# Layer-norm statistics of a hybrid block: row sums taken with the residual additions, squared distances on ScalarE

## The chip, the cores and the metric

The kernel runs on one core of a Trainium2 chip. The metric is the device time of one launch in microseconds. Before the change three runs gave a median of 2213.21 us (2209.37 to 2219.28).

The engines are named as in the profile: PE is TensorE, PEld its weight loads, DVE is VectorE, ACT is ScalarE, POOL is GpSimd, SP is SyncE (it issues DMAs only). Each takes its own instructions strictly in order and waits for the others by semaphores.

## The reference

Input x has 16 batches of 512 tokens with 256 features, float32. One block of a hybrid network is applied, with four residual steps and a layer norm (no weights) in front of each:

```python
x = x + attention(layernorm(x))   # 16 heads, causal, RMS norm first, returns xn + out
x = x + ffn(layernorm(x))         # base + shared low-rank + top 2 of 6 routed low-rank
x = x + ssm(layernorm(x))         # conv of 4 taps, silu, softplus, scan with 16 states, gate
x = x + ffn(layernorm(x))

def layernorm(x, eps=1e-05):
    m = mean(x, -1); v = var(x, -1)
    return (x - m) / sqrt(v + eps)
```

The change concerns the mean and variance of the second, third and fourth of these layer norms.

## The kernel before, in words

A batch is held as a tile X of 128 partitions by 4 token blocks by 256 features; five such slots rotate. All engines walk through one common calendar. A group of four heads is a step q; a step has UN = 10 units p, and a unit has two places, 2(10q + p) and one more. Four groups make a batch, so the calendar repeats every 80 places. The tables PE_AT, ACT_AT, DVE_AT, POOL_AT and SP_AT say at which place, counted from the start of a batch's attention, an engine does each piece of side work for that batch (its projections, norms, feed-forward, state-space part). `due` (L239) picks the batch whose turn it is, `side_work` of each engine runs down its list. Some five batches are in flight: attention of one, feed-forward of the one before, the scan of an earlier one. The places are only an order of instructions on each queue. Time follows from the semaphores.

Between the side work stands the fixed work of each unit. PE makes scores twice: for the row maxima (L357, L359), 14 units ahead, into two PSUM banks that DVE reduces (L970 to L975), and for the exponentials (L380, L382), into two banks that ACT reads (L767); then products with the values (L405). DVE runs one scan of the state (L1090) and one product with the row C (L1097) four times per step; ACT makes the decays for them (L864), POOL the input products (L1262), and POOL's DMA adds each state's product to y (L1269). Two more PSUM banks, MA and MB, serve all side work; BANK says which result lies in which, and a bank is filled again only when its reader has freed it.

A layer norm goes through three engines. There are four kinds: q before attention, f and l before the first and the last feed-forward, s before the state-space part. For f, s and l:

- DVE adds the PSUM result of the step before to X, two token blocks at a time (`add_to_x`, L1016 to L1020: places add_x1, add_up0, add_x3).
- `moments_of_sum` (L1022) waits for both halves and calls `moments` (L1003): four bn_stats, four bn_aggr, then the variance with epsilon into `va` and the negative mean into `ng` (L1013, L1014). Its places are stats_f, stats_s and stats_l.
- POOL's `rsqrt` (L1227) raises `va` to the power -0.5 into `rs` (L1229) and multiplies by `ng` into `nm` (L1231).
- ACT's `normalise` (L774) writes X times rs plus nm for four token blocks (L777). PE then transposes.

Kind q has its statistics from DVE as well, and they stay there. The last feed-forward's result is added by `add_to_x` (add_up1) and stored by SP (`store`, L722), which waits for both halves. SP's queue also carries the loads of stacked q and k parts (`stack`, L687, three thirds at the first three units of a step) and the broadcast rows of B (`load_b`).

Of the kernel before, what the change touches and what calls it, by code (L numbers as in the profile page):

```python
# [56 lines left out]
def hybrid_block(nc, x, norm_w, wqk_t, bqk_c, wv_t, bv, wo_t, bo, conv_w, conv_b, wd_t, bd, wbc_t,  # L57
# [32 lines left out]
    PRODUCT_AT = {1: 0, 4: 1, 6: 2, 8: 3}  # L90
# [6 lines left out]
    PE_AT = {"xn": (-76, -71), "qk00": (-52, -50, -48), "qk01": (-49, -47, -44), "v": (-29, -34),  # L97
# [4 lines left out]
    BANK = {"xn": (0, 1), "qk00": 0, "qk01": 1, "v": (1, 1), "qk10": 0, "qk11": 1, "ao": (1, 1), "x1": (1, 0),  # L102
            "turn0": (1, 1), "low0": 1, "hw0": 1, "up0": (1, 0), "xs": (1, 0), "conv": (1, 1), "gate": (1, 0),
            "bc": 1, "dt": (0, 0), "x3": (1, 0), "turn1": (1, 0), "low1": 0, "hw1": 0, "up1": (1, 0)}
    ACT_AT = {"norm_q": -97, "norm_f": 103, "exp0": 116, "norm_s": 131, "softplus": 152, "decays": 160,
# [4 lines left out]
    DVE_AT = {"add_x1": (94, 96), "stats_f": 98, "in0": 111, "out0": 117, "add_up0": (125, 125), "stats_s": 127,  # L110
              "silu": 143, "delta": 155, "gated": 246, "add_x3": (251, 251), "stats_l": 252, "in1": 265, "out1": 267,
              "add_up1": (279, 282), "stats_q": -100}
    POOL_AT = {"weigh": -57, "residual": -57, "rsqrt_f": 99, "rsqrt_s": 122, "rsqrt_q": -104, "inputs": 151,
               "rsqrt_l": 253, "low": (111, 268)}
    SP_AT = {"parts": (-42, -3), "load_x": -109, "store_b": 144, "store": 280}
# [3 lines left out]
    with ctx:  # L119
# [77 lines left out]
        nm = sb("nm", [P, 4, TB])  # L197
        low = sb("low", [P, 2, TB, LR])
# [558 lines left out]
        def _(act):  # L757
# [115 lines left out]
            def side_work(now):  # L873
# [46 lines left out]
                if (a := due(now, ACT_AT["norm_q"])) >= 0:  # L920
                    act.wait_ge(res_done.sem, res_done.at(a - 1))
                    normalise(a, KIND_Q, X[:, a % XS, :, :], tok_q)
                if (a := due(now, ACT_AT["norm_f"])) >= 0:
                    normalise(a, KIND_F, X[:, a % XS, :, :], tok_f)
                if (a := due(now, ACT_AT["exp0"])) >= 0:
                    exp_logits(a, 0)
                if (a := due(now, ACT_AT["norm_s"])) >= 0:
# [3 lines left out]
                if (a := due(now, ACT_AT["decays"])) >= 0:  # L931
                    decays(a, 0)
                    decays(a, 1)
                if (a := due(now, ACT_AT["norm_l"])) >= 0:
# [26 lines left out]
        def _(dve):  # L961
# [41 lines left out]
            def moments(b, kind, mul, add):  # L1003
                src = X[:, b % XS, :, :]
# [145 lines left out]
            def side_work(now):  # L1150
# [3 lines left out]
                for j in range(2):  # L1154
                    if (a := due(now, DVE_AT["add_x3"][j])) >= 0:
                        add_to_x(a, side["x3", j], ("x3", a, j), j)
                if (a := due(now, DVE_AT["stats_l"])) >= 0:
                    moments_of_sum(a, KIND_L, ("x3",))
# [7 lines left out]
                for j in range(2):  # L1166
                    if (a := due(now, DVE_AT["add_x1"][j])) >= 0:
                        if j == 0:
                            dve.wait_ge(res_done.sem, res_done.at(a))
                        add_to_x(a, side["x1", j], ("x1", a, j), j)  # L1170
                if (a := due(now, DVE_AT["stats_f"])) >= 0:
                    moments_of_sum(a, KIND_F, ("x1",))
# [4 lines left out]
                for j in range(2):  # L1177
                    if (a := due(now, DVE_AT["add_up0"][j])) >= 0:
                        add_to_x(a, side["up", 0, j], ("up", a, 0, j), j)
                if (a := due(now, DVE_AT["stats_s"])) >= 0:  # L1180
                    moments_of_sum(a, KIND_S, ("up", 0))
# [22 lines left out]
            for q in range(FIRST, END):  # L1204
# [3 lines left out]
                for p in range(UN):  # L1208
                    if 0 <= UN * q + p + LM < UN * NQ:
                        maximum(UN * q + p + LM)  # L1210
                    if p == HEADS_DVE and 0 <= q - 1 < NQ:
                        head_norm(q - 1)
# [5 lines left out]
                    if p == 6 and 0 <= q + 1 < NQ:  # L1218
# [145 lines left out]
```

## Time and profile before

| | |
|---|---|
| median of three runs | 2213.21 us |
| the profiled execution | 2220.23 us |
| its span, first to last instruction | 2218.4 us |
| mean granted TensorE clock | 0.934 of full |
| PE busy | 1819.8 us, 82% |
| DVE busy | 1856.9 us, 84% |
| ACT busy | 1289.4 us, 58% |
| POOL busy | 1171.1 us, 53% |

Busy time is the sum of an engine's instruction durations, in which short overlaps of neighbours count twice. So a slot, the distance between two starts, is often shorter than a duration. A wait names the instruction that was kept waiting, then the one whose end released it. Line numbers are those of the kernel before.

### The profile page before, as it was taken

The numbers are of one execution on the slowest core, as the hardware profiler recorded it, in microseconds if no ns is written. First come the engines' busy times: TensorE is split into PE (matmuls) and PEld (weight loads), VectorE is DVE, ScalarE is ACT, GpSimd is POOL, SyncE is SP. The second block draws the span as 40 slices with busy tenths as digits, with TensorE's granted clock in tenths as the row PEclk, the third lists the DMA queues.
The fourth block names the chain that finished last, engine by engine and source line by source line (L and its number), as shares of the span: only waits on it lengthen the run. The fifth ranks groups of instructions, "written<-read, shape, count | busy, mean of one in ns | idle before, by whom it ended". The sixth has DMA issues, their size and how long they took to land.

```text
span 2218.4 us, 32220 instructions
## 1 busy us (share of the span) xinstructions
PE 1819.8 (82%) x10881; PEld 1082.1 (49%) x10912; DVE 1856.9 (84%) x2760; ACT 1289.4 (58%) x2260; POOL 1171.1 (53%) x994
## 2 busy tenths in 40 slices
PE   5789787888889798888888788888978888877775
PEld 2445444546355454645455454545545463535343
DVE  5444798989899897989899898989889897978784
ACT  2446566566756657575665656576565657463531
POOL 1110665656455564647465464756556474556682
PEclk8999899999989999999999899999999999888988
DMA  4312576667657665666767666666766666651110
GB/s 114 91 49 68 120 152 145 145 140 152 130 125 155 140 153 124 146 137 137 154 134 147 143 145 136 140 130 142 151 143 152 129 149 129 124 120 53 48 62 14
DMA packets 186054, 275.56 MB, mean 124 GB/s; under 512 B 33554, under 2 KB 125731, under 8 KB 185891
## 3 DMA queue, kind: packets, MB, share of 16 engines
q1 hardware_dynamic: 155650, 163.40, 28.9%
q0 software_dynamic: 30240, 110.11, 26.8%
q8 instruction: 87, 1.43, 0.3%
q14 instruction: 77, 0.62, 0.1%
HBM read 128.72 MB, written 34.08 MB: 73 GB/s over the span
## 4 chain that ended last, share of the span: by engine, by line
PE 31%; DVE 26%; DMA 14%; issue 12%; ACT 8%; POOL 5%; SPq 3%; DVEq 0%; POOLq 0%; ACTq 0%
DVE hc L1090 9%; PE bank L313 7%; DMA y<-hc 5%; DVE hc L1097 4%; POOL inp L1262 4%; PE bank L322 4%; DMA sk<-qk_parts 3%; DMA qk_parts<-parts 3%; PE bank L503 3%; PE bank L357 2%; PE bank L486 2%; PE bank L405 2%; PE bank L380 2%; DVE mall L975 2%; SPq L698 2%
## 5 line engine op out<-in xcount | busy, mean ns | idle before, releaser
L1262 POOL TENSOR_TENSOR inp<-u,b_all 128x512 f32<-128x512 f32 x512 | 731.8, 1469 | 333.7 <-DVE hc L1090 222.0
L1090 DVE TENSOR_TENSOR_SCAN hc<-dec,inp 128x1024 f32<-128x1024 f32 x256 | 672.4, 2627 | 20.7 <-ACT dec L864 19.3
L767 ACT ACTIVATE pt<-bank 128x512 f32<-128x512 f32 x640 | 375.2, 598 | 253.0 <-PE bank L382 251.1
L357 PE MATMUL bank<-sk,sq 96*128 96x512 bf16 (+3 forms) x1024 | 281.7, 314 | 131.9 <-DVE mall L973 52.3
L1269 POOL DMA_DIRECT2D y<-hc x210 | 186.0, 886 | 353.9 <-DMA y<-hc 162.5
L864 ACT ACTIVATE dec<-dt,a_neg 128x511 f32<-128x511 f32 x512 | 338.5, 719 | 39.4 <-DVE hc L1090 39.4
L1097 DVE TENSOR_TENSOR hc<-hc,bank 128x1024 f32<-128x1024 f32 x242 | 293.3, 1212 | 25.5 <-PE bank L542 24.9
L380 PE MATMUL bank<-sq,sk 98*128 98x512 bf16 (+3 forms) x1024 | 276.4, 308 | 15.3 <-DMA sq<-hlt 10.3
L973 DVE TENSOR_REDUCE mall<-bank 128x1 f32<-128x512 f32 x256 | 172.5, 674 | 138.6 <-PE bank L359 138.4
L357 PEld LDWEIGHTS bank<-sk,sq 96*128 96x128 bf16 x1024 | 102.9, 100 | 279.4 <-DVE mall L973 80.0
L313 PE MATMUL bank<-xt_q,wqk 128*128 128x512 f32 x256 | 153.6, 731 | 73.8 <-ACT bcs L844 67.9
L359 PE MATMUL bank<-mask_qk,ident_bf 128*128 128x128 bf16 x1024 | 199.9, 226 | 0.0
L382 PE MATMUL bank<-mask_kq,ident_bf 128*128 128x128 bf16 x1024 | 197.6, 224 | 0.0
L975 DVE TENSOR_REDUCE mall<-bank 128x4 f32<-128x512 f32 x256 | 172.9, 675 | 19.2 <-PE bank L359 18.9
L405 PE MATMUL bank<-pt,v_sb 128*32 128x512 f32 (+3 forms) x2048 | 186.3, 460 | 0.0
L1229 POOL TENSOR_TENSOR rs<-va,half 128x4 f32<-128x4 f32 x64 | 88.1, 1376 | 185.4 <-DVE ng L1014 185.3
L786 ACT ACTIVATE parts<-bank,bqk 128x512 bf16<-128x512 f32 x192 | 131.2, 688 | 93.7 <-PE bank L313 87.1
L380 PEld LDWEIGHTS bank<-sq,sk 98*128 98x128 bf16 x1024 | 103.7, 101 | 80.2 <-issue 19.6
L542 PE MATMUL bank<-bcs,onehot 96*128 96x512 bf16 x256 | 102.7, 401 | 35.3 <-DVE hc L1097 34.5
L359 PEld LDWEIGHTS bank<-mask_qk,ident_bf 128*128 128x128 bf16 x1024 | 103.5, 101 | 46.2 <-issue 28.4
L382 PEld LDWEIGHTS bank<-mask_kq,ident_bf 128*128 128x128 bf16 x1024 | 103.5, 101 | 42.2 <-issue 25.9
L1019 DVE TENSOR_TENSOR X<-bank,X 128x512 f32<-128x512 f32 x128 | 85.5, 678 | 45.5 <-PE bank L322 25.6
(152 smaller groups left out, 3271.6 us busy)
## 6 DMA issues: line engine op xcount, KB each, us to landing
y<-hc POOLq DMA_DIRECT2D x210, 512.0 KB, 5.5
b_all<-b_kept SPq DMA_DIRECT2D x256, 256.0 KB, 4.3
qk_parts<-parts SPq DMA_DIRECT2D x96, 256.0 KB, 3.1
sq<-qk_parts SPq DMA_DIRECT2D x384, 64.0 KB, 3.4
sk<-qk_parts SPq DMA_DIRECT2D x384, 64.0 KB, 3.6
X<-in_x SPq DMA_DIRECT2D x16, 512.0 KB, 7.9
out<-X SPq DMA_DIRECT2D x16, 512.0 KB, 3.0
sq<-hlt SPq DMA_DIRECT2D x256, 2.0 KB
```

The source lines that it names most:

```text
L313: last = mm(dst[:, :], w[:, c, g * P:(g + 1) * P], src[:, c, :], start=(c == 0), stop=(c == C - 1))
L357: mm(dst[:, o:o + n], sq[0:KS, slot, h, qb * P:(qb + 1) * P], sk[0:KS, slot, h, 0:n], start=True, stop=False)
L359: return mm(dst[:, o + n - P:o + n], ident_bf[:, :], mask_qk[:, :], start=False, stop=True)
L380: mm(dst[:, o:o + n], sk[:, slot, h, kb * P:(kb + 1) * P], sq[:, slot, h, kb * P:T], start=True, stop=False)
L382: return mm(dst[:, o:o + P], ident_bf[:, :], mask_kq[:, :], start=False, stop=True)
L405: last = mm(pv_bank[VW * i:VW * (i + 1), kb * P:T], values_of(a, kb, first + i), pt[:, n % PT, at:at + T - kb * P], start=start, stop=stop ...
L767: A(pt[:, n % PT, :], score_bank[unit % 2][:, :], ACT.Exp).then_inc(exp_done.sem, 1)
L864: last = A(dec[:, n % 2, c, 1:T], dt[:, c, 1:T], ACT.Exp, scale=a_neg[:, c, n:n + 1])
L975: V.tensor_reduce(mall[:, w, h, 0:4], max_bank[m % 2][:, :].rearrange("p (k n) -> p k n", k=TB), AXX, ALU.max).then_inc(mx_done.sem, 1)
L1090: V.tensor_tensor_scan(h, d, v, 0.0, ALU.mult, ALU.add).then_inc(scan_done.sem, 1)
L1097: V.tensor_tensor(hc[:, k % HC, :, :] if n or s >= LATE else y[:, s % 2, :, :], hc[:, k % HC, :, :], spread_bank[:, None, :].to_broadcast( ...
L1262: last = G.tensor_tensor(inp[:, n % 2, c, :], u[:, c, :], b_all[:, k % 3, :], ALU.mult)
```

## The change

The additions for f, s and l now take each token block by itself, in an operation that also sums the row (`add_and_sum`). ACT makes the negative mean from the sums and then the sum of squared distances from it, with an accumulating Square (`squares`); it waits for both additions first. POOL divides by 256 and adds epsilon before the power. The statistics of kind q, and the last addition (add_up1), are as before. `squares` writes its elementwise output into the tile that the norm overwrites. The places and banks of the side work are new.

```diff
+            def squares(b, kind, name, junk):
+                for j in range(2):
+                    m = side[*name, j]
+                    act.wait_ge(m.free, m.at(name[0], b, *name[1:], j))
+                A(ng[:, kind, :], sums[:, kind, :], ACT.Copy, scale=-1.0 / D).then_inc(act_own.sem, 1)
+                act.wait_ge(act_own.sem, act_own.one())
+                for tb in range(TB):
+                    last = A(junk[:, tb, :], X[:, b % XS, tb, :], ACT.Square, bias=ng[:, kind, tb:tb + 1],
+                             accum_out=va[:, kind, tb:tb + 1])
+                last.then_inc(var[kind].sem, 1)
...
-            def moments_of_sum(b, kind, name):
-                for j in range(2):
-                    m = side[*name, j]
-                    dve.wait_ge(m.free, m.at(name[0], b, *name[1:], j))
-                moments(b, kind, 1.0, 1e-5)
+            def add_and_sum(b, m, name, j, kind):
+                dve.wait_ge(m.full, m.at(*name))
+                for t in range(2):
+                    row = X[:, b % XS, 2 * j + t, :]
+                    last = V.scalar_tensor_tensor(row, m.tile[:, t * D:(t + 1) * D], 1.0, row, ALU.mult, ALU.add,
+                                                  accum_out=sums[:, kind, 2 * j + t:2 * j + t + 1])
+                last.then_inc(m.free, 1)
...
             def rsqrt(b, kind):
                 pool.wait_ge(var[kind].sem, var[kind].at(b))
+                if kind != KIND_Q:
+                    G.tensor_scalar(va[:, kind, :], va[:, kind, :], 1.0 / D, 1e-5, ALU.mult,
+                                    ALU.add).then_inc(pool_own.sem, 1)
+                    pool.wait_ge(pool_own.sem, pool_own.one())
...
-    PRODUCT_AT = {1: 0, 4: 1, 6: 2, 8: 3}
+    PRODUCT_AT = {1: 0, 3: 1, 6: 2, 8: 3}
```

The tables of places, in the entries that the prediction speaks of or that moved most:

| entry | before | after |
|---|---|---|
| ACT square_f, square_s, square_l | none | 98, 125, 252 |
| DVE stats_f, stats_s, stats_l | 98, 127, 252 | gone |
| DVE add_x1, add_x3 | (94, 96), (251, 251) | same |
| DVE add_up0 | (125, 125) | (124, 124) |
| POOL rsqrt_f, rsqrt_s, rsqrt_l | 99, 122, 253 | 97, 122, 254 |
| POOL weigh, residual | -57, -57 | -56, -45 |
| POOL inputs | 151 | 153 |
| PE v | (-29, -34) | (-26, -32) |
| PE turn1 | (260, 262) | (262, 264) |
| PE up0 | (125, 126) | (123, 125) |
| DVE add_up1 | (279, 282) | (277, 280) |
| SP store, load_x, store_b | 280, -109, 144 | 278, -112, 146 |

Most others of attention's projections and both feed-forwards move by one to three; conv, gate, bc, dt, silu and delta stay. The banks of v, ao, x1 and x3 change for one half each. `finish_maxima` stands at the same place as before.

## Rows read from the trace of the kernel before

**Rows 1.** The page, busy time and share by engine, whole span.

```profile
PE 1819.8 (82%) x10881; PEld 1082.1 (49%) x10912; DVE 1856.9 (84%) x2760; ACT 1289.4 (58%) x2260; POOL 1171.1 (53%) x994
```

**Rows 2.** Busy time by stretches: length, PE, PEld, DVE, ACT, POOL, clock, DMA.

```profile
903.00:1029.00 126.00, 106.66 (x672) 65.47 (x673) 116.23 (x171) 80.15 (x141) 73.68 (x64) 0.96 0.67 143
...
1785.00:1911.00 126.00, 106.80 (x664) 64.51 (x666) 112.04 (x161) 77.84 (x137) 71.40 (x62) 0.95 0.66 139
...
925.00:945.00 20.00, 19.68 (x146) 13.89 (x145) 19.61 (x27) 12.13 (x23) 11.02 (x9) 1.00 0.81 181
...
957.00:992.00 35.00, 28.88 (x160) 13.53 (x159) 27.19 (x28) 29.05 (x48) 16.48 (x15) 0.95 0.55 109
```

**Rows 3.** Waits of DVE, 903 to 1029 us: us in total, times, longest.

```profile
DVE mall L973 <- PE bank L359: 4.5, 2, 3.4
DVE mall L970 <- PE bank L359: 1.8, 2, 1.5
```

**Rows 4.** Waits of PE in the same period.

```profile
PE bank L313 <- ACT bcs L844: 4.9, 1, 4.9
PE bank L357 <- DVE mall L973: 3.4, 3, 2.3
PE bank L357 <- DVE mall L975: 2.8, 3, 1.4
```

**Rows 5.** DVE in order of time: start us, us, engine, line, operation.

```profile
1000.66 0.42 DVE L999 TENSOR_TENSOR ao<-bank,rc 128x256 f32<-128x256 f32 x1
1001.01 1.21 DVE L1097 TENSOR_TENSOR hc<-hc,bank 128x1024 f32<-128x1024 f32 x1
...
1014.98 0.68 DVE L1019 TENSOR_TENSOR X<-bank,X 128x512 f32<-128x512 f32 x1
1015.58 1.21 DVE L1097 TENSOR_TENSOR hc<-hc,bank 128x1024 f32<-128x1024 f32 x1
...
1017.31 1.40 DVE L1006 BATCH_NORM_STATS2 st<-X 128x6 f32<-128x256 f32 x4
...
1019.23 0.16 DVE L1014 TENSOR_SCALAR ng<-mv 128x4 f32<-128x4 f32 x1
1019.30 0.69 DVE L970 TENSOR_REDUCE mall<-bank 128x2 f32<-128x512 f32 x1
```

**Rows 6.** By line: durations in ns, min/median/max, then first and last start.

```profile
L1019 DVE TENSOR_TENSOR X<-bank,X x128: 656/680/694, 144.9 to 2214.2; 128x512 f32<-128x512 f32 x128
...
L1108 DVE SCALAR_TENSOR_TENSOR y<-gate,bank x4: 655/678/686, 2110.5 to 2182.9; 128x512 f32<-128x512 f32 x4
```

**Rows 7.** ACT: in order of time, its largest wait of the period, one line's durations.

```profile
936.53 0.59 ACT L793 COPY v_sb<-bank 128x512 f32<-128x512 f32 x1 [5.68 <-PE bank L322]
...
1016.50 0.57 ACT L767 ACTIVATE pt<-bank 128x512 f32<-128x512 f32 x1
...
1022.21 2.07 ACT L777 ACTIVATE tok_f<-X,nm,rs 128x256 f32<-128x256 f32 x4 [0.15 <-POOL nm L1231]
...
ACT pt L767 <- PE bank L382: 15.0, 10, 4.9
...
L947 ACT ACTIVATE a_neg<-a_neg x1: 229/229/229, 36.0 to 36.0; 128x32 f32<-128x32 f32 x1
```

**Rows 8.** POOL, by line: the power and the product of the norm.

```profile
L1229 POOL TENSOR_TENSOR rs<-va,half x64: 1007/1034/2934, 7.1 to 2190.8; 128x4 f32<-128x4 f32 x64
...
L1231 POOL TENSOR_TENSOR nm<-ng,rs x64: 202/203/2251, 8.2 to 2191.8; 128x4 f32<-128x4 f32 x64
```

**Rows 9.** The chain of waits, at the start and at the end.

```profile
148.29 1.41 DVE st L1006 x4
...
2187.78 0.70 DVE X L1019
2188.58 1.42 DVE st L1006 x4
```

**Rows 10.** POOL in order of time, behind the last statistics.

```profile
2191.84 0.20 POOL L1231 TENSOR_TENSOR nm<-ng,rs 128x4 f32<-128x4 f32 x1
```

More of the change, by code:

```diff
@@ L96, in hybrid_block @@
     FRAME = 2 * UN * NG
-    PE_AT = {"xn": (-76, -71), "qk00": (-52, -50, -48), "qk01": (-49, -47, -44), "v": (-29, -34),
[4 rows of a table removed]
-    BANK = {"xn": (0, 1), "qk00": 0, "qk01": 1, "v": (1, 1), "qk10": 0, "qk11": 1, "ao": (1, 1), "x1": (1, 0),
-            "turn0": (1, 1), "low0": 1, "hw0": 1, "up0": (1, 0), "xs": (1, 0), "conv": (1, 1), "gate": (1, 0),
-            "bc": 1, "dt": (0, 0), "x3": (1, 0), "turn1": (1, 0), "low1": 0, "hw1": 0, "up1": (1, 0)}
-    ACT_AT = {"norm_q": -97, "norm_f": 103, "exp0": 116, "norm_s": 131, "softplus": 152, "decays": 160,
[4 rows of a table removed]
[L110 to L115, printed above, removed]
+    PE_AT = {"xn": (-76, -70), "qk00": (-52, -50, -47), "qk01": (-50, -47, -43), "v": (-26, -32),
[4 rows of a table added]
+    BANK = {"xn": (0, 1), "qk00": 0, "qk01": 1, "v": (1, 0), "qk10": 0, "qk11": 1, "ao": (0, 1), "x1": (0, 0),
+            "turn0": (1, 1), "low0": 1, "hw0": 1, "up0": (1, 0), "xs": (1, 0), "conv": (1, 1), "gate": (1, 0),
+            "bc": 1, "dt": (0, 0), "x3": (0, 1), "turn1": (1, 0), "low1": 0, "hw1": 0, "up1": (1, 0)}
+    ACT_AT = {"square_f": 98, "square_s": 125, "square_l": 252, "norm_q": -94, "norm_f": 103, "exp0": 116,
+              "norm_s": 132, "softplus": 152, "decays": 160, "norm_l": 257, "exp1": 266, "xn": (-77, -71),
[4 rows of a table added]
+    DVE_AT = {"add_x1": (94, 96), "in0": 109, "out0": 116, "add_up0": (124, 124), "silu": 143, "delta": 155,
+              "gated": 246, "add_x3": (251, 251), "in1": 265, "out1": 266, "add_up1": (277, 280), "stats_q": -100}
+    POOL_AT = {"weigh": -56, "residual": -45, "rsqrt_f": 97, "rsqrt_s": 122, "rsqrt_q": -102, "inputs": 153,
+               "rsqrt_l": 254, "low": (111, 266)}
+    SP_AT = {"parts": (-42, -3), "load_x": -112, "store_b": 146, "store": 278}
+    FINISH = 13
     HEADS_PE, HEADS_DVE = 4, 4
@@ L197, in hybrid_block @@
         nm = sb("nm", [P, 4, TB])
+        sums = sb("sums", [P, 4, TB])
         low = sb("low", [P, 2, TB, LR])
@@ L922, in side_work @@
                     normalise(a, KIND_Q, X[:, a % XS, :, :], tok_q)
+                if (a := due(now, ACT_AT["square_f"])) >= 0:
+                    squares(a, KIND_F, ("x1",), tok_f)
                 if (a := due(now, ACT_AT["norm_f"])) >= 0:
@@ L926, in side_work @@
                     exp_logits(a, 0)
+                if (a := due(now, ACT_AT["square_s"])) >= 0:
+                    squares(a, KIND_S, ("up", 0), tok_f)
                 if (a := due(now, ACT_AT["norm_s"])) >= 0:
@@ L933, in side_work @@
                     decays(a, 1)
+                if (a := due(now, ACT_AT["square_l"])) >= 0:
+                    squares(a, KIND_L, ("x3",), y_tok(a))
                 if (a := due(now, ACT_AT["norm_l"])) >= 0:
@@ L1155, in side_work @@
                     if (a := due(now, DVE_AT["add_x3"][j])) >= 0:
-                        add_to_x(a, side["x3", j], ("x3", a, j), j)
-                if (a := due(now, DVE_AT["stats_l"])) >= 0:
-                    moments_of_sum(a, KIND_L, ("x3",))
+                        add_and_sum(a, side["x3", j], ("x3", a, j), j, KIND_L)
                 if (a := due(now, DVE_AT["in1"])) >= 0:
@@ L1169, in side_work @@
                             dve.wait_ge(res_done.sem, res_done.at(a))
[L1170 to L1172 removed]
+                        add_and_sum(a, side["x1", j], ("x1", a, j), j, KIND_F)
                 if (a := due(now, DVE_AT["in0"])) >= 0:
@@ L1210, in _ @@
                         maximum(UN * q + p + LM)
+                    if FINISH == 2 * p and 0 <= q + 1 < NQ:
+                        finish_maxima(q + 1)
                     if p == HEADS_DVE and 0 <= q - 1 < NQ:
@@ L1217, in _ @@
                         product(k + PRODUCT_AT[p])
-                    if p == 6 and 0 <= q + 1 < NQ:
+                    if FINISH == 2 * p + 1 and 0 <= q + 1 < NQ:
                         finish_maxima(q + 1)
```

4 lines of the change are left out of this document (1 added, 3 removed), and 16 rows, old and new, of tables (ACT_AT, PE_AT).

## The prediction

> **What bounds the kernel now.** I read the page's totals first: VectorE (DVE) is busy 84% of the span, TensorE (PE) 82%, ScalarE (ACT) 58%, GpSimd (POOL) 53% [rows 1]. An average over a start, a steady part and an end does not say who sets the time, so the table by stretches comes next. From 273 to 2037 us the span falls into 14 equal periods of 126 us, one per batch; the sixth and the thirteenth are shown [rows 2]. Each has DVE busy 112 to 116 us of 126, PE about 107. The list of waits of one period (903 to 1029) tells more: DVE sat idle for PE 4.5 and 1.8 us, the two largest of six entries that sum to 8.2 us [rows 3]. It is occupied 93% of the time. PE in its turn waited 3.4 + 2.8 = 6.2 us for DVE's maximum reductions, and once 4.9 us for ACT's cast of B and C [rows 4]. So the two engines hold each other through two PSUM banks. Which one leads changes within the period. From 957 to 992 (convolution, gate, delta) DVE has only 27.2 us of work in 35; from 925 to 945 both are full, PE with 19.7 of 20; in the rest DVE is the full one [rows 2]. The three blocks that the change touches lie in the stretches where DVE is full: l and f between 1004 and 1020 [rows 5], s inside 925 to 945.
>
> **DVE: what goes.** A block of statistics is four BATCH_NORM_STATS2, four aggregates and two small scalings. Their durations overlap, so I count starts: the f block starts at 1017.31 and the next reduction at 1019.30, 1.99 us. The two additions before it each take a slot of 0.60 us (1014.98 to 1015.58) [rows 5]. Before: 1.99 + 1.20 = 3.19 us per block, three blocks per batch.
>
> **DVE: what comes.** Four additions of 128x256 with a row sum. A 128x256 operation from PSUM takes a slot of 0.35 us (1000.66 to 1001.01) [rows 5]; SCALAR_TENSOR_TENSOR from PSUM runs at the speed of the plain addition, 678 against 680 ns for 512 elements [rows 6]. The addition never exceeded 694 ns [rows 6], so it doesn't collide with POOL, and I expect that of its new form too. The price of the sum isn't in this trace. Lower bound: a small operation's slot, 0.07 us (1019.23 to 1019.30), which makes 0.42 each. Upper bound at full streaming rate: no overlap at all, 0.42 + 0.16 = 0.58 us each [rows 5]. I take 0.15, near the duration of a small operation, so 0.50 each and 2.0 per block. DVE saves 3.19 - 2.0 = 1.2 us per block (0.87 to 1.51), 3.6 per batch.
>
> The Trainium skill (VectorE: DVE Perf Modes, "Two Vector instructions with no wait between them") says that an operation with an accumulator output is two instructions, and the same page's "Rules for kernel authors" advises keeping the number of operations small. By it two additions become eight instructions. That is the small slot I add; if each read waited for its addition to drain the block would take 2.32 us and the batch would save 2.6 instead of 3.6.
>
> **How much of it shows.** The f and l savings (2.4 us per period) lie where DVE is full and PE waits 6.2 us in the period for DVE's maxima, so they can pass through entire. The s saving lies just where PE is full as well [rows 2]; I count half, 0.6. Sum 3.0.
>
> **ACT: what comes.** Per block a copy of 128x4 (the nearest row, 128x32, is 0.23 us [rows 7]) and four squares with sums. Four scaled rows of the same shape take 2.07 us [rows 7]; with about 0.1 each for the sum, 2.7 us per block, 8.1 per batch (bounds 1.6, if the simpler operands help, to 3.1, if every sum is a separate 0.23 us). ACT waits 15.0 us per period for PE before its exponentials [rows 7] and is busy 80 of 126 [rows 2], so most of this is covered. But ACT's queue is in order, and two things stand behind the squares: exponentials, which free the score banks for PE, and copies out of PSUM. For f, ACT is at place 98 when it starts the exponential at 1016.50 [rows 7]; the second addition is done at 1014.98 + 0.68 [rows 5], so the squares don't wait, but that exponential starts 2.7 us later, and PE can go on only until its other score bank is full. For s, ACT had been idle 5.68 us before its copy at 936.53 [rows 7]; squares that start when the additions are through, about 935, push that copy and the exponential behind it by 1 to 1.5. For l the squares come in a like pause of ACT. I charge 0.2 us per period: 3.0 becomes 2.8. The cover gone would be the slow rival below.
>
> **POOL.** One more scalar operation on 128x4 per block: bounds 0.20 (the small product's usual time) and 2.25 (its longest, behind a scan); I take 0.3 [rows 8]. POOL's wait moves from DVE's statistics to ACT's squares, at places 97, 122 and 254, between the same input products as before, so what is queued behind it (input products for the scan, additions of states by DMA) meets about the same delay. No wait of DVE for POOL is among those of the period.
>
> **The places.** Most shifts are one to three of 80 places. Three could matter. The residual (two additions of POOL) moves 12 places behind the weighing and no longer forms one block with it before input products. The store moves from 280 to 278 on SyncE: it now waits for the last addition at DVE's 280 instead of 282, with all three thirds of the next stack behind it instead of two, but a unit sooner. DVE's product 1 comes one unit earlier, which lets its C row be spread sooner. The dense stretch from 957 to 992 keeps its places, so its idle DVE time stays. I count the places as nothing, minus 2 to plus 2 us per period, and carry both ends.
>
> **Ends.** Where the chain of waits runs through a norm, its length counts. In the last one the second addition starts at 2187.78 and ends 0.70 later, the shift is ready at 2191.84 + 0.20: 3.6 us from sum to shift [rows 9, 10]. After: 0.25 more for the additions, 2.7 on ACT, 1.7 on POOL (0.3 + 1.0 + 0.2 and gaps [rows 8]), 0.3 between engines: 5.0, so 1.4 longer. The chain passes five such blocks in the start and the end (three at the end, two at the start; the first and the last are shown) [rows 9]: 5 x 1.4 = 7 us lost.
>
> **Sum.** 14 x 2.8 = 39, less 7, is 32 us. Against the profiled execution, 2220.2 us (span 2218.4 and 1.8 around it), 2188; that execution lay 7.0 above the median of 2213.2, so the median becomes 2181.
>
> **Rivals.**
> *Everything passes and the places help (0.18).* All 3.6 us show, and the new places close 2 us more of the 8 us that DVE idles per period: 14 x 5.6 - 7 = 71, 2142. For it: the places are the only part that can touch DVE's idle time. Against: the largest idle pieces stand where nothing moves.
> *The sum is dear, or PE takes over (0.14).* An addition that streams at half rate costs another 0.256 us (680 - 424 ns for 256 elements [rows 5, 6]): 0.77 each, 3.1 per block, and the saving is 0.1 per block. 14 x 0.3 less 7 gives 2216. PE as the full engine in all three places would give the same figure. Against it: all elementwise rows here run at one rate, and PE's waits for DVE are real. The Trainium skill (Vector Engine (DVE) Microarchitecture Reference, "Points that are easy to get wrong") has a rule that would do this, half throughput for scalar_tensor_tensor with two sources in SBUF that are not bf16; one source here is PSUM, and no run here shows the summing form.
> *ACT's queue becomes the bound (0.18), slower.* Mechanism: the squares wait in order for DVE's additions and then hold 2.7 us; the exponential behind them comes late, PE stops at its second score bank, and the maxima that DVE needs come late as well. It decides from 2.8 us of stall per period, 0.9 per block. If each block costs 1.6 us (the squares less about one microsecond of cover), it is 4.8 - 3.0 = 1.8 us per period, 25 in all, and 7 of the ends: 2245. For it: in the f block the second addition ends only 0.8 us before ACT comes to its squares [rows 5, 7]. Against: 15 us of waiting in ACT per period.
> *The sum above (0.50).* 2181, its own range 2155 to 2200.
>
> **How the numbers follow.** A difference under 0.5% (11 us) can't be told from none: faster is below 2202, slower above 2224. Faster: all of the fast rival, 0.46 of the sum's 0.50 and a little of the third, 0.67. Slower: nearly all of the slow rival and a little of the dear one, 0.19. Same: 0.14. The range must reach from just under the fast rival to beyond the dear one and into the slow one: 2136 to 2232.
>
> **What would show it.** Right: periods of about 123 us; a DVE addition group of 256 with a slot near 0.5 and DVE's busy time down by some 60 us; ACT up by 110 to 130 us; PE's waits for maxima shorter, DVE's wait for PE longer. The ends longer by some 7 us. Wrong: summing additions over 0.7 us; PE waiting for ACT's exponentials or ACT for DVE's additions by more than 2 us per period; more table loads on ACT than before, which would mean that the square changes the table; scans that wait for POOL.

## The result, and the profile after

The kernel with the change took 2258.1 us in the median of four runs (2251.1 to 2263.0), the kernel before 2213.6 beside it: a ratio of 1.0197, 95% interval 1.0161 to 1.0233. It is slower by 2.0%. The prediction said 2181 us, 1.5% faster, with 2136 to 2232 as its range; both sign and range were missed. No rival's mechanism proved to be the main one either.

The page of the kernel after, busy time and share by engine, and some of its groups (line, engine, operation, count | busy us, mean ns of one | idle before, and what ended it):

```profile
PE 1831.8 (81%) x10881; PEld 1093.5 (49%) x10912; DVE 1769.5 (79%) x2568; ACT 1398.9 (62%) x2692; POOL 1164.6 (52%) x1042
...
L359 PE MATMUL bank<-sk,sq 96*128 96x512 bf16 (+3 forms) x1024 | 282.2, 314 | 183.8 <-DMA sk<-qk_parts 80.7
...
L1121 DVE TENSOR_TENSOR hc<-hc,bank 128x1024 f32<-128x1024 f32 x242 | 293.7, 1214 | 74.4 <-PE bank L544 72.6
...
L1048 DVE SCALAR_TENSOR_TENSOR X<-bank,X 128x256 f32<-128x256 f32 x192 | 72.4, 418 | 63.5 <-PE bank L324 41.8
```

Against [rows 1]: DVE did 87.4 us less, ACT 109.5 more, POOL 6.5 less, and the profiled span is 30.9 longer (2249.3 against 2218.4). The work moved as it was meant to, and the time went the other way. (Busy time on the page is the length of the stretches in which an engine is busy: overlaps count once, and not twice as was said above. The first L309 row under experiment 5 shows it: 256 instructions with a mean of 304 ns, 42.3 us busy.)

In the kernel before, the groups that answer to the second and third line were these:

```profile
L357 PE MATMUL bank<-sk,sq 96*128 96x512 bf16 (+3 forms) x1024 | 281.7, 314 | 131.9 <-DVE mall L973 52.3
...
L1097 DVE TENSOR_TENSOR hc<-hc,bank 128x1024 f32<-128x1024 f32 x242 | 293.3, 1212 | 25.5 <-PE bank L542 24.9
```

Two waits are new or grew. PE's first score product of a step waits 80.7 us in all for the load of `sk` (before: 36.4, experiment 2). DVE's product with C waits 72.6 us for PE where it had waited 24.9: what DVE saved turned into waiting for PE. This second wait isn't the loss: with the store put right (experiment 2) it still is 68.3 us, and the time is 2.2% shorter.

Busy time by stretches, kernel after (length, PE, PEld, DVE, ACT, POOL, clock, DMA share, GB/s), the steady part and one period:

```profile
273.00:2065.00 1792.00, 1495.65 (x9198) 904.38 (x9223) 1506.88 (x2150) 1196.69 (x2314) 1011.47 (x912) 0.94 0.64 137
945.00:1073.00 128.00, 105.63 (x639) 64.21 (x640) 103.86 (x151) 83.61 (x163) 70.97 (x65) 0.91 0.61 133
```

and the steady part of the kernel before:

```profile
273.00:2037.00 1764.00, 1481.25 (x9145) 891.47 (x9169) 1579.89 (x2310) 1095.90 (x1928) 1010.02 (x862) 0.94 0.64 138
```

Over 14 periods DVE's work fell from 1579.9 to 1506.9, 73 us, and its idle time rose from 184 to 285, 101 us. The difference, 28 us, is the loss. From the second s norm to the last but one (13 periods, the starts of its small copy or scaling, 303.35 to 1976.40 after and 301.74 to 1951.61 before) a period grew from 126.9 to 128.7 us, 23 us in all; of the remaining 8 of the 31, 1.6 lie ahead of this stretch and 6.1 behind it.

**Where PE waits.** SyncE's queue in the kernel after (SPq is SyncE issuing a DMA; L727 is the store, L700 a load of stacked parts), then PE's waits from 938 to 956 us:

```profile
938.33 0.38 SPq L727 DMA_DIRECT2D out<-X  x1
938.75 0.51 SPq L721 DMA_DIRECT2D b_all<-b_kept  x1
939.36 0.87 SPq L700 DMA_DIRECT2D sq<-qk_parts  x1
940.28 1.26 SPq L700 DMA_DIRECT2D sk<-qk_parts  x1
...
949.75 0.59 SPq L700 DMA_DIRECT2D sk<-qk_parts  x1
```

```profile
PE bank L359 <- DMA sk<-qk_parts: 5.0, 1, 5.0
```

The same place in the kernel before:

```profile
923.77 0.33 SPq L698 DMA_DIRECT2D sq<-qk_parts  x1
...
925.08 0.43 SPq L698 DMA_DIRECT2D sk<-qk_parts  x1
928.27 0.40 SPq L725 DMA_DIRECT2D out<-X  x1
928.78 0.44 SPq L698 DMA_DIRECT2D sq<-qk_parts  x1
```

Before, the first third of the next stack left 4.5 us ahead of the store (923.77, 928.27), and the store waited for DVE's last addition with two thirds, eight loads, behind it. After, the store comes first and all twelve loads stand behind it, from 939.36 to 949.75. PE's first score product of a step waits for all twelve (`max_unit`), so what counts for it is when the last one lands. That is 6.13 us after its issue, and the chain of waits of the kernel after passes through it:

```profile
939.36 6.80 DMA sq<-qk_parts
...
949.75 6.13 DMA sk<-qk_parts
```

Summed over the trace, PE's waits for these loads that end within 25 us behind a store are 49.0 us in the kernel after (twelve waits) and none in the kernel before.

**The new operations.** DVE, ACT and POOL by line, durations in ns (min/median/max), kernel after:

```profile
L1048 DVE SCALAR_TENSOR_TENSOR X<-bank,X x192: 391/419/426, 149.1 to 2218.3; 128x256 f32<-128x256 f32 x192
L1048 DVE DVE_READ_ACCUMULATOR X<-bank,X x192: 75/83/85, 149.5 to 2218.6; 128x1 f32 x192
...
L791 ACT ACTIVATE tok_f<-X,ng x128: 491/492/511, 153.2 to 2088.4; 128x256 f32<-128x256 f32 x128
L791 ACT ACTIVATION_READ_ACCUMULATOR tok_f<-X,ng x128: 185/186/192, 153.6 to 2088.8; 128x1 f32 x128
...
L1250 POOL TENSOR_SCALAR va<-va x48: 189/191/2013, 155.4 to 2221.2; 128x4 f32<-128x4 f32 x48
```

and DVE in order of time at one pair of additions:

```profile
1028.34 0.42 DVE L1048 SCALAR_TENSOR_TENSOR X<-bank,X 128x256 f32<-128x256 f32 x1
1028.69 0.08 DVE L1048 DVE_READ_ACCUMULATOR X<-bank,X 128x1 f32 x1
1028.69 2.29 DVE L1114 TENSOR_TENSOR_SCAN hc<-dec,inp 128x1024 f32<-128x1024 f32 x1
```

The addition's slot is 0.35 us with its sum, just what another 128x256 operation from PSUM took without one [rows 5]: the read of the accumulator starts with the next instruction and costs nothing that shows. The norm's part on DVE is now 4 x 0.35 = 1.4 us instead of 3.19.

### The profile page after: what moved, and what is told of

The parts are those of the page before. It is cut to its first block, busy times and chain, and to the rows that moved or that the text cites. A ratio compares the mean times of both kernels' runs of the same rounds, so it can differ in the third digit from the quotient of the medians.

```text
span 2249.3 us, 32508 instructions
## 1 busy us (share of the span) xinstructions
PE 1831.8 (81%) x10881; PEld 1093.5 (49%) x10912; DVE 1769.5 (79%) x2568; ACT 1398.9 (62%) x2692; POOL 1164.6 (52%) x1042
## 4 chain that ended last, share of the span: by engine, by line
PE 35%; DVE 20%; ACT 16%; DMA 13%; issue 8%; SPq 4%; POOL 3%; ACTq 0%; POOLq 0%; DVEq 0%
PE bank L315 6%; DMA sk<-qk_parts 6%; DVE hc L1114 6%; PE bank L505 5%; PE bank L324 3%; SPq L700 3%; PE bank L359 3%; ACT dec L878 3%; PE bank L407 3%; DVE hc L1121 3%; PE bank L488 3%; DMA sq<-qk_parts 3%; ACT pt L769 3%; PE bank L382 2%; DVE diff L1063 2%
## 5 line engine op out<-in xcount | busy, mean ns | idle before, releaser
L1286 POOL TENSOR_TENSOR inp<-u,b_all 128x512 f32<-128x512 f32 x512 | 720.1, 1440 | 410.0 <-DVE hc L1114 302.9
L1114 DVE TENSOR_TENSOR_SCAN hc<-dec,inp 128x1024 f32<-128x1024 f32 x256 | 630.9, 2464 | 32.9 <-ACT dec L878 31.3
L359 PE MATMUL bank<-sk,sq 96*128 96x512 bf16 (+3 forms) x1024 | 282.2, 314 | 183.8 <-DMA sk<-qk_parts 80.7
L1121 DVE TENSOR_TENSOR hc<-hc,bank 128x1024 f32<-128x1024 f32 x242 | 293.7, 1214 | 74.4 <-PE bank L544 72.6
L382 PE MATMUL bank<-sq,sk 98*128 98x512 bf16 (+3 forms) x1024 | 281.3, 313 | 21.4 <-ACT pt L769 14.9
L1048 DVE SCALAR_TENSOR_TENSOR X<-bank,X 128x256 f32<-128x256 f32 x192 | 72.4, 418 | 63.5 <-PE bank L324 41.8
```

The lines of the kernel that those rows point to most:

```text
L359: mm(dst[:, o:o + n], sq[0:KS, slot, h, qb * P:(qb + 1) * P], sk[0:KS, slot, h, 0:n], start=True, stop=False)
L382: mm(dst[:, o:o + n], sk[:, slot, h, kb * P:(kb + 1) * P], sq[:, slot, h, kb * P:T], start=True, stop=False)
L1114: V.tensor_tensor_scan(h, d, v, 0.0, ALU.mult, ALU.add).then_inc(scan_done.sem, 1)
L1121: V.tensor_tensor(hc[:, k % HC, :, :] if n or s >= LATE else y[:, s % 2, :, :], hc[:, k % HC, :, :], spread_bank[:, None, :].to_broadcast( ...
L1286: last = G.tensor_tensor(inp[:, n % 2, c, :], u[:, c, :], b_all[:, k % 3, :], ALU.mult)
```

## The experiments

In the diffs, "after" and "before" are the two kernels. All ratios are to the kernel before, with their 95% intervals.

**1. The two halves apart.** The statistics of after with all places and banks of before:

```
-"square_f": 98, "square_s": 125, "square_l": 252, ... (all places of after)
+"square_f": 98, "square_s": 127, "square_l": 252, ... (all places and banks of before)
```

> The new statistics at the old places and banks: row sums with the additions, squares on ScalarE at the places where VectorE had its statistics (98, 127, 252), product 1 at unit 4. If the places made the kernel slow (theory P), this is faster than before: VectorE saves 1.0 to 1.3 us per block, 2175 to 2205 us. If the squares in ScalarE's ordered queue made it slow (theory Q: they wait 70.6 us in all for VectorE's additions and hold the exponentials), it is as slow as the changed kernel, 2245 to 2265 us.

Measured: 2290.7 us, 1.0334 (1.0308 to 1.0360). The statistics alone, at the old places, lose 3.3%.

The reverse, the statistics of before (at 98, 125 and 252) with the places and banks of after:

> The old statistics on VectorE (at 98, 125, 252) with the new places and banks. Theory P: slower than before by more than the changed kernel, since VectorE also keeps its 87 us of work: 2260 to 2300 us. Theory Q: near the kernel before, 2205 to 2225 us.

Measured: 2247.1 us, 1.0125 (1.0091 to 1.0158). This half carries the store at 278 with it. Each half alone is slower, and together they lose 2.0%, less than the sum of 4.6. Neither of the two theories gave these figures: the first run lies above both of its ranges, the second between them. So "the places count as nothing" is wrong both ways.

**2. The store.** In after:

```
-SP_AT = {"parts": (-42, -3), "load_x": -112, "store_b": 146, "store": 278}
+SP_AT = {"parts": (-42, -3), "load_x": -112, "store_b": 146, "store": 280}
```

> The changed kernel with the store back at 280, behind the first third of the next stack on SyncE's queue. TensorE's wait for the stacked parts before a maximum was 80.7 us against 36.4 before. If the store ahead of all three thirds causes that (theory S), the wait falls back to about 40 us and the time by 20 to 40 us, to 2220 to 2240. If the wait only shows that TensorE arrives early after time lost elsewhere, the time stays within 5 us of 2258.

Measured: 2213.5 us, 0.9977 (0.9952 to 1.0002). One number undoes the whole loss. PE's wait for `sk` falls from 80.7 to 33.6 us:

```profile
PE bank L359 <- DMA sk<-qk_parts: 33.6, 13, 8.0
```

The other way round, 278 in before:

> The kernel before with one entry changed: the store at 278 instead of 280. Theory S (the store ahead of the first third of the stack holds the stack): slower than before by 25 to 45 us, 2240 to 2260, and TensorE's wait for the stacked parts up from 36 to 60 or more. If the store matters only together with the new statistics, within 5 us of 2214.

Measured: 2254.2 us, 1.0152 (1.0107 to 1.0196), and the same wait rises from 36.4 to 84.7 us (kernel before, then this one):

```profile
PE bank L357 <- DMA sk<-qk_parts: 36.4, 16, 7.8
```

```profile
PE bank L357 <- DMA sk<-qk_parts: 84.7, 25, 7.9
```

with the order of after on SyncE:

```profile
937.57 0.38 SPq L725 DMA_DIRECT2D out<-X  x1
938.00 0.51 SPq L719 DMA_DIRECT2D b_all<-b_kept  x1
938.62 0.86 SPq L698 DMA_DIRECT2D sq<-qk_parts  x1
```

Then the store behind all three thirds, at 284, in after and in before:

> The changed kernel with the store at 284, behind all three thirds of the next stack. By theory S SyncE then never holds a stack for VectorE's last addition, and TensorE's wait for stacked parts is at most the 33.6 us that it is at 280. If the place at 280 still costs something, 2195 to 2210 us; if 280 was enough, within 5 us of store280 (0.998 of before).

> The kernel before with the store at 284. Same reasoning: 2195 to 2212 if the place at 280 cost something before too, within 5 us of 2214 if not.

Measured: 2202.0 us, 0.9947 (0.9929 to 0.9966), and 2197.2 us, 0.9926 (0.9897 to 0.9955). In before it is a gain, and where it comes from stays open (PE's wait for `sk` is 41.2 us there, no less than 36.4); in after it can't be told from 280, as the intervals overlap.

The waits that end within 25 us behind a store follow the place. In after they are 49.0 us at 278, 7.1 at 280 and none at 284; in before none at 280 and 52.8 at 278. So the store's place is shown as the main cause: against 280 it costs 2.2% in after and 1.5% in before. Two things change with it, the third that goes ahead and how many places the store stands ahead of the addition it waits for. Before at 280 and after at 278 both have it two places ahead (add_up1 at 282 and 280) and differ by none against 49.0 us, which points to the third; no run parts the two in one kernel.

**3. The statistics, with the store put right.** Old statistics at the new places, store at 280 and at 284:

> The old statistics on VectorE with the new places and the store at 280. The store should give back some 45 us here too: 2247 to about 2203. Against 2213.5 with the new statistics this would mean that the new statistics cost 10 us by themselves though VectorE does less. If VectorE's saved work counts, this is slower than 2213.5, by 20 us or more.

> The old statistics in all three blocks, new places, store at 284. If the new statistics are worth what they were at store 280 (0.93% of the time), this is 20 us slower than store284 (2202), about 2222. If they are worth nothing once the store is out of the way, within 5 us of 2202.

Measured: 2231.3 us, 1.0071 (1.0041 to 1.0102), and 2228.9 us, 1.0041 (1.0013 to 1.0070). Against these the new statistics gain 0.9% (0.9977 and 0.9947), some 20 us, where the forecast had 32. The first expectation had the store give back 45 us here too. It gave back 0.5% (1.0125 in `places_new` to 1.0071), which the intervals can't tell from nothing, although PE's wait for `sk` fell from 62.5 to 27.3 us. So what the store costs depends on the rest of the kernel: 2.2% and 1.5% in the two kernels of this document, 0.5% with the old statistics at the new places. The other new places, with the old statistics, cost 0.7% at store 280 (1.0071) and 1.2% at 284 (1.0041 against 0.9926).

**4. What the squares hold.** The four squares of each block are left out: one copy-like operation on the sums takes their place, so the variance isn't the reference's. At the new places with store 280, and at the old places:

```
-for tb in range(TB):
-    last = A(junk[:, tb, :], X[...], ACT.Square, bias=..., accum_out=va[...])
+last = A(va[:, kind, :], sums[:, kind, :], ACT.Abs)
```

> The changed kernel with the store at 280, and without the four squares of each block: one Abs of the sums stands for them, so this computes another variance; all waits stay. It takes 2.1 us of ScalarE work and its holding of the queue away, three times a batch. Theory Q (the squares hold exponentials that TensorE and then VectorE need): faster than with the squares (2213.5) by 20 to 60 us, 2155 to 2195. If the squares are covered by ScalarE's 15 us of waiting per batch: within 8 us of 2213.

> The new statistics at the old places (2290.7) with one Abs of the sums in the place of the four squares, so another variance is computed. At the new places the squares are worth 14 us. Theory Q at old places (the squares stand where they hold exponentials): it falls by 60 us or more, to 2230 or below. If it falls by 10 to 25 only, the squares are not why the old places are bad for the new statistics.

Measured: 2199.7 us, 0.9911 (0.9880 to 0.9942), and 2242.1 us, 1.0117 (1.0093 to 1.0141). At the new places the squares cost 0.7% (from 0.9977), 14 us, or about 1.0 per period. At the old places they cost 2.2%, 48 us. ACT's work is the same in both; what stands behind it differs. At the new places PE's wait for exponentials falls from 11.3 to 4.6 us without the squares. At the old ones PE's wait for the f and s norms' tokens falls from 39.2 to 17.9 us, that for exponentials only from 13.2 to 9.0.

**5. Which old place hurts the new statistics.** The product in the old places moved to unit 3, and the s block in the new order (squares 125, norm 132, additions at 124, PE's up0 at 123 and 125):

```
-PRODUCT_AT = {1: 0, 4: 1, 6: 2, 8: 3}
+PRODUCT_AT = {1: 0, 3: 1, 6: 2, 8: 3}
```

> The new statistics at the old places with the second product at unit 3. At the new places unit 4 instead of 3 cost 0.6% (14 us). If VectorE's product and its spread row are the order that the old places lack, 2290 falls to 2260 or less; if the gain belongs to the whole table, it stays within 10 us of 2290.

> The new statistics at the old places (2290.7), with block s alone as in the new tables: squares at 125, norm at 132, additions at 124, up0 at (123, 125). If GpSimd's wait at 122 for the later squares (at 127), with input products and state additions queued behind it, is what the old places suffer from, it falls by 25 us or more. If not, it stays within 10 us of 2290.

Measured: 2264.8 us, 1.0218 (1.0195 to 1.0241), and 2264.5 us, 1.0198 (1.0149 to 1.0248). Each alone takes back a third or more of the 3.3%. In the second PE's transposes wait less long for the normalised tokens; their group in comp_old, then in comp_old_s:

```profile
L309 PE MATMUL bank<-ident,tok_f 128*128 128x128 f32 x256 | 42.3, 304 | 50.7 <-ACT tok_f L779 39.2 <-ACT xt_f L813 11.6
```

```profile
L309 PE MATMUL bank<-ident,tok_f 128*128 128x128 f32 x256 | 39.5, 289 | 27.4 <-ACT tok_f L779 15.9 <-ACT xt_f L813 11.6
```

In the old order the square's place was 127 and its normalisation's 131; the longer path (squares, one more POOL operation) no longer fitted into these four places, two units. The expectation's own reason, POOL waiting at 122 for the later squares, isn't parted from this: POOL's waits for squares fell as well, from 110.0 to 93.2 us. And the product at unit 4 in after, store 280:

> The changed kernel with the store at 280 and the second product back at unit 4. VectorE waits for TensorE's spread C row ahead of its products 68 us in all, against 25 before. If the early unit causes that wait and it counts, the wait falls to about 30 us and the time by 10 to 30 us under 2213.5. If VectorE merely waits elsewhere instead, within 6 us.

Measured: 2227.6 us, 1.0035 (1.0018 to 1.0051) against 0.9977: the earlier product is worth 0.6% at the new places and 1.2% at the old ones, with the new statistics in both. The expectation, that DVE's wait for the C row would fall and the time with it, failed in both: the wait is 70.9 us against 68.3, and the time rose.

**6. The weighing.** In after (store 278), the weighing and the residual both back to -57:

```
-"weigh": -56, "residual": -45
+"weigh": -57, "residual": -57
```

> The changed kernel with GpSimd's weighing and residual back at -57, side by side. In the changed kernel single small VectorE operations of the router took 5.7 to 5.8 us while GpSimd worked through weighing and input products without a pause; before they took at most 1.3. If those stretches cost time (theory G), the small operations fall back under 1.5 us and the time falls by 10 to 40 us. If their cost is only shifted from the scans, the scans grow by about 40 us and the time stays within 8 us of 2258.

Measured: 2266.0 us, 1.0221 (1.0186 to 1.0255) against 1.0197. The intervals overlap: not a cause of the loss.

**7. Which block gains.** At the new places with store 284, the old statistics for s alone, and for f and l alone:

> As store284, but block s has its old statistics on VectorE (at 125), f and l the new ones. The prediction gave s half of the worth of the others, because VectorE and TensorE are both full there: then this is about 4 us slower than store284. If the squares of s hold ScalarE where it matters (it waited 2.4 us per batch for VectorE's additions ahead of them), this is faster than store284, by 5 us or more.

> As store284, but blocks f and l have their old statistics on VectorE (98 and 252), s the new ones. By the prediction these two carry four fifths of the gain: about 16 us slower than store284. If the gain is in s alone, within 5 us of store284.

Measured: 2253.4 us, 1.0164 (1.0127 to 1.0200), and 2183.1 us, 0.9848 (0.9811 to 0.9885). With runs 2 and 3 this is a table of two by two:

```
                  f and l old   f and l new
s old               1.0041        1.0164
s new               0.9848        0.9947
```

The s block gains 1.9 to 2.2%, f and l lose 1.0 to 1.2%, and within the intervals the two effects add. Both expectations missed: s alone back in its old form was to cost 4 us or to gain 5, and costs 51; f and l were to cost 16 us or nothing, and gain 19. The lower left corner is the fastest of all kernels run: 1.5% under before and 3.4% under after. The store at 284 alone takes before to 0.9926, so about half of the 1.5% needs none of the new statistics.

The traces of the four show what goes with each effect (waits and busy time in us; the clock is the granted share in the profiled execution, a mean of stretches at 2.4 and at 1.2 GHz):

| | PE waits for DVE's maxima | PE waits for ACT's gate copies and exponentials | PE busy | clock |
|---|---|---|---|---|
| s old, f and l old | 129.3 | 13.8 | 1851.0 | 0.918 |
| s new, f and l old | 102.8 | 13.8 | 1827.8 | 0.929 |
| s old, f and l new | 145.1 | 27.0 | 1866.0 | 0.909 |
| s new, f and l new | 113.9 | 28.3 | 1821.6 | 0.930 |

The largest wait for maxima with everything old, then with s new; the wait for exponentials with everything new, then with f and l old:

```profile
PE bank L357 <- DVE mall L973: 68.9, 61, 3.7
```

```profile
PE bank L359 <- DVE mall L989: 46.4, 47, 2.2
```

```profile
PE bank L382 <- ACT pt L769: 11.6, 19, 2.7
```

```profile
PE bank L382 <- ACT pt L769: 5.1, 4, 2.7
```

With the new statistics of s, PE waits 26 and 31 us less for DVE, and it is busy 23 and 44 us less with the same instructions, at a higher clock. With those of f and l its waits for ACT double. The clock is a rival that no run parts from the rest: time and clock go together within one kernel too (the one with everything old took 2205.3 us at 0.925 and 2233.9 at 0.914), and which is the cause isn't shown. The kernel before has 0.934 in its profiled execution, so part of what the new places cost with the old statistics may be the clock as well.

**8. What goes with the loss of f and l.** One part of it is above: PE waits some 14 us longer for ACT, which now has the squares. Another shows on DVE. In fl_old284 the router's small operations (24 and 144 elements) are short, in store284 some are very long. DVE groups of store284, then of fl_old284:

```profile
L1063 DVE TENSOR_TENSOR diff<-ex 128x144 f32<-128x144 f32 x32 | 72.3, 2258 | 1.5 <-ACT ex L822 1.5
...
L1058 DVE TENSOR_TENSOR lg<-low,red 128x24 f32<-128x24 f32 x32 | 23.1, 722 | 1.1
```

```profile
L1060 DVE TENSOR_TENSOR lg<-low,red 128x24 f32<-128x24 f32 x32 | 19.2, 600 | 1.1
...
L1065 DVE TENSOR_TENSOR diff<-ex 128x144 f32<-128x144 f32 x32 | 11.7, 367 | 0.9 <-ACT ex L822 0.9
```

POOL and DVE of the kernel after in order of time show one such case (the two fences are the same stretch):

```profile
1038.11 4.48 POOL L1286 TENSOR_TENSOR inp<-u,b_all 128x512 f32<-128x512 f32 x2
1042.53 0.91 POOL L1293 DMA_DIRECT2D y<-hc  x1
1043.19 3.06 POOL L1269 TENSOR_TENSOR tok_q<-tok_q,w_row 128x256 f32<-128x256 f32 x4
1045.94 2.74 POOL L1286 TENSOR_TENSOR inp<-u,b_all 128x512 f32<-128x512 f32 x2
```

```profile
1043.05 5.67 DVE L1058 TENSOR_TENSOR lg<-low,red 128x24 f32<-128x24 f32 x1
1048.65 0.68 DVE L993 TENSOR_REDUCE mall<-bank 128x1 f32<-128x512 f32 x1
```

An operation of 24 elements lasts 5.67 us, until the last of POOL's six products ends at 1048.68; a maximum reduction stands behind it. The Trainium skill (SBUF — State Buffer, "SBUF: two separate sides") has a rule for such a wait: VectorE and GpSimd share a pair of ports, which one of them holds for a whole instruction where the DVE operation has two SBUF inputs, and the other blocks. The trace fits it, as both inputs of this operation are in SBUF, but the wait here spans six GpSimd instructions in a row and not one. Another row of the kernel before looks like a wait for one alone. The product with the gate (L1103, both inputs in SBUF) takes 1.21 us with no GpSimd product beside it, and 1.99 where one had started 0.36 us before it and ended 0.91 us into it:

```profile
L1103 DVE SCALAR_TENSOR_TENSOR y<-gate,y x14: 1207/1986/1992, 359.7 to 2007.1; 128x1024 f32<-128x1024 f32 x14
```

What decides between the two cases isn't shown.

To part this from the squares' hold on ACT, the weighing was moved three places later in store284 (its expectation says four, by mistake), and the same in fl_old284 as a control:

```
-"weigh": -56, "residual": -45
+"weigh": -53, "residual": -45
```

> The kernel after with the store at 284 (2202 us) and the weighing additions at -53 instead of their place in the kernel after, nothing else. Theory: what the new statistics of the first and last norm cost is VectorE's small router difference held about 5 us behind GpSimd's weighing and input products that run back to back; with the weighing four units later the difference's mean falls from 2258 ns to under 1000 ns and the time to between 2177 and 2192. Rival: the wait is hidden and the cost comes from ScalarE's in-order squares; then the time stays within 6 us of 2202, whatever the difference's mean. Second rival: the weighing only meets the scans instead, and the time rises.

> The kernel after with the store at 284, the first and last norm's statistics as before (2183 us), and the weighing additions at -53. Control for the run above: here the router difference took 367 ns already, so by the theory the time stays within 6 us of 2183; if the later weighing is good or bad by itself, this kernel moves as the other does.

Measured: 2204.1 us, 0.9946 (0.9925 to 0.9967), and 2202.9 us, 0.9943 (0.9928 to 0.9959). The first didn't take the wait away but moved it; the control made one where none had been, and became slower. The same two groups in weigh53_284 and in fl_old_weigh53:

```profile
L1058 DVE TENSOR_TENSOR lg<-low,red 128x24 f32<-128x24 f32 x32 | 58.4, 1825 | 1.1
L1063 DVE TENSOR_TENSOR diff<-ex 128x144 f32<-128x144 f32 x32 | 42.7, 1334 | 1.5 <-ACT ex L822 1.5
```

```profile
L1060 DVE TENSOR_TENSOR lg<-low,red 128x24 f32<-128x24 f32 x32 | 49.4, 1544 | 1.1
...
L1065 DVE TENSOR_TENSOR diff<-ex 128x144 f32<-128x144 f32 x32 | 19.5, 609 | 0.9 <-ACT ex L822 0.9
```

Together the two groups take 31 us in fl_old284 (2183 us), 69 in fl_old_weigh53 (2203), 95 in store284 (2202) and 101 in weigh53_284 (2204). Both expectations failed as numbers: the first kernel was to fall, the second to stay. What they show is this: with the statistics and ACT's work untouched, moving POOL's weighing alone raises the small operations by 38 us and the time by 20 (0.9848 to 0.9943). The held operations are one possible reason for that; the move delays the weighing itself as well. Against a price in proportion: store284 has 26 us more of them than fl_old_weigh53 and the same time, and `weigh_old` has 22 us less of them than the kernel after (70 against 92) and isn't faster. The squares have a price of their own: without them, and with 96 us of held operations in either, experiment 4 gained 0.7%. How the loss of f and l divides between the two stays open; a kernel with the squares and without the held operations was not found.

## Why the prediction was wrong

**The places (the step that failed).** The prediction saw the store: "it now waits for the last addition at DVE's 280 instead of 282, with all three thirds of the next stack behind it instead of two, but a unit sooner". Then it counted this as nothing, with 2 us per period as the bound. By the ratios it costs 2.2% in after, 49 us or 3.5 per period, and 1.5% in before, 34 us or 2.4 per period. The prediction named no wait for it. The runs show one: PE's first score product of a step needs all twelve loads, and its waits for them behind a store grow from 7.1 to 49.0 us in after and from none to 52.8 in before. With a third ahead, eight loads follow the store on SyncE's queue instead of twelve. "A unit sooner" gave nothing, since the stack's loads, and not the store, were what PE needed.

The rest of the places was not zero either, nor a number of its own: with the old statistics they cost 0.7 to 1.2%, with the new ones they gain 3.6% (1.0334 to 0.9977, the store at 280 in both). Nor was the store: it costs 0.5% with the old statistics at the new places. Computation and places had to be priced as one thing.

**DVE.** Right in kind, too small in size: the summing addition takes a slot of 0.35 us where 0.50 was taken, under the lower bound of 0.42. A block saves 1.8 us instead of 1.2, DVE's total 87 instead of some 60. So the rival of the dear sum is refuted. (Two slips in the recorded sums change nothing: 0.50 + 0.256 is 0.76 and not 0.77, and ACT's upper bound with the copy is 0.23 + 2.07 + 4 x 0.23 = 3.2 and not 3.1.)

**How much of it shows.** The rule that f and l pass through entire and s by half came out the other way round. s gains about 2% (some 3 us per period), more than DVE's 1.8 us in it; f and l lose 1%. The rule looked at how full DVE and PE are over 20 us, and took PE's being full around s as a reason why the saving would be lost. What the runs show instead: with the new statistics of s PE's waits for maxima fall by 26 and 31 us, and it is busy 23 and 44 us less, at a higher clock. The clock wasn't in the forecast at all, and whether it is a cause or follows stays open. That the norm's length as a path counts in s isn't borne out: PE's waits for the tokens of the f and s norms are 4.5 us with the old s and 6.9 with the new (f and l new in both), and 10.9 and 13.2 with f and l old. For f and l "DVE is full" said only that DVE has work, not that this work is what PE waits for; and ACT's new work there has a price, 14 us of PE's waits.

**ACT.** Busy +109.5 us (110 to 130 forecast), a block 0.2 + 4 x 0.49 = 2.2 us instead of 2.7, no more table loads. The charge for in-order waiting was 0.2 us per period; the runs without squares bound it at 1.0 with the store at 280, squares and all. The slow rival put the stall at 4.8 and gave 2245: near the measured 2258 in number, and not the mechanism. ACT's squares do cost much at the old places, 48 us, but more through PE's transposes waiting for the normalisation (39.2 us, without squares 17.9) than through the exponentials (13.2, without squares 9.0).

**POOL.** "What is queued behind it meets about the same delay": for the scans this held; DVE waited 1.3 us for input products before a scan in either kernel (for decays, which ACT makes, 31.3 instead of 19.3). What it left out is that POOL's work, looked at as something that waits, can also be something that DVE waits for (experiment 8). The scalar operation itself takes 191 ns in the median, the mean is 680 (0.3 taken).

**The ends.** In the last norm the second pair of additions starts at 2217.91 and the shift is ready at 2222.55 + 0.20, 4.84 us later; before it was 4.26 (2187.78 to 2192.04 [rows 9, 10]). So this norm is 0.6 us longer, 1.4 forecast; from the end of the additions it is 4.07 against 3.56, and 4.07 against 3.97 in the first f norm. The count of periods gives some 8 us for start and end together, 7 forecast, but five norms of 0.1 to 0.6 us more don't make that: the number was met by luck, and where the rest comes from stays open.

**The sum.** Put together with the store put right, the forecast's own subject, the new statistics at the new places, gives 0.2% (store at 280, not told from none) or 0.5% (at 284) where 1.5% was forecast. s alone, the part that it rated least, gives 1.5%, again the forecast's number by another way, and by luck: the store at 284 alone gives before about half as much.

## What to carry to other kernels

When places move together with the work, walk each in-order queue and ask of every instruction that waits what now stands behind it: here one store moved by two places, ahead of four loads, cost 2.2% where the new arithmetic gave 0.9%. Treat the time from the last input to the consumer as the price of a step on a path, and its busy time as the price only on an engine that others wait for. Where a change has several like parts, run them one by one: the best kernel here leaves two of the three parts out. And compare the granted clock of the kernels before a gain is put down to work or to waits.

## What the runs showed of the hardware

- The row sum of a DVE addition is free in this pattern: a separate accumulator read of 83 ns, starting with the next instruction, and a slot of 0.35 us, as a 128x256 operation from PSUM has without it.
- On ACT the read of 186 ns overlaps the squares in part: a square of 128x256 with its sum takes a slot of 0.49 us, four of them 1.96.
- A DVE operation of 24 elements with both inputs in SBUF lasted 5.67 us while GpSimd ran products back to back (1043.05 to 1048.72) and ended with them; at its shortest the same operation took 0.18 us. The scans, on the other hand, were shorter in the mean than in the kernel before: 2457 ns in store284 against 2627.
- The same PE instructions took between 1821.6 and 1866.0 us of busy time in the four kernels of experiment 7, the least at a mean granted clock of 0.930 and the most at 0.909.
